# The first x turned into four PSUM banks by halves, and one idle matmul behind the turning where two stood

## The reference, cut to what matters

```python
k = x @ W_lat + b_lat                      # 256 -> 128, one latent shared by all heads, also the values
q = (x @ W_d + b_d) split into 16 heads of 128
att = softmax(causal(q @ k.T / sqrt(128)))
x = layernorm(x + (att @ k, heads joined) @ W_proj + b_proj)
scores = x @ router_weight + router_bias   # the best half of the rows of each batch
x = layernorm(x + scatter(sigmoid(score) * ffn(chosen rows)))
```

## Time and profile before

| what | value |
|---|---|
| median of 3 runs | 280.72 us (280.70 to 280.82) |
| the profiled execution's own time | 280.79 us |
| its span, first to last instruction | 279.1 us |
| PE busy | 271.6 us, 97% of the span |
| DVE busy | 218.8 us, 78% |
| ACT busy | 212.1 us, 76% |
| POOL busy | 153.9 us, 55% |

### The profile page before, as it was taken

One profiled execution on the slowest core, in us unless ns is written; L12 is line 12 of the kernel. 1 busy time (PEld: TensorE's weight loads), 2 busy tenths in 40 slices (PEclk: granted clock), 3 DMA queues, 4 the chain that ended last, 5 costly groups with the idle time before them and its releaser, 6 DMA issues.

```text
span 279.1 us, 6206 instructions
## 1 busy us (share of the span) xinstructions
PE 271.6 (97%) x1885; PEld 247.2 (89%) x1885; DVE 218.8 (78%) x701; ACT 212.1 (76%) x578; POOL 153.9 (55%) x214
## 2 busy tenths in 40 slices
PE   8999999999999999999999999999999999999991
PEld 4878999999999998999999999999999999999990
DVE  2698777777777777788789888899988887779882
ACT  3689877777787778887787877787777778879471
POOL 6468444444443336555666866665657847238652
PEclk9999999999999999999999999999999999999997
DMA  6593111011101111111111111110112200020151
GB/s 184 137 305 112 39 40 34 27 33 38 34 24 36 38 39 38 40 38 42 38 38 40 38 41 38 39 37 22 38 38 79 78 21 21 1 77 1 58 171 38
DMA packets 18842, 15.53 MB, mean 56 GB/s; under 512 B 1641, under 2 KB 18178, under 8 KB 18818
## 3 DMA queue, kind: packets, MB, share of 16 engines
q1 hardware_dynamic: 18242, 13.65, 16.8%
q0 software_dynamic: 576, 1.58, 1.6%
HBM read 12.60 MB, written 2.63 MB: 55 GB/s over the span
## 4 chain that ended last, share of the span: by engine, by line
PE 97%; DVE 0%; POOLq 0%; issue 0%; ACT 0%; DVEq 0%
PE bank L412 21%; PE bank L414 20%; PE bank L413 20%; PE bank L547 9%; PE ps_out L412 7%; PE ps_out L413 6%; PE ps_out L414 6%; PE bank L527 3%; PE bank L637 3%; PE bank L470 1%; PE bank L424 1%; POOLq L60 0%; PE bank L676 0%; PE bank L678 0%; PE bank L557 0%
## 5 line engine op out<-in xcount | busy, mean ns | idle before, releaser
L841 ACT ACTIVATE probs<-probs,negmax 128x512 f32<-128x512 f32 (+3 forms) x128 | 72.6, 576 | 5.7 <-DVE negmax L1026 4.3
L1384 POOL TENSOR_TENSOR wd_hi<-wd_raw,zero 128x256 fp32r<-128x256 f32 x31 | 23.7, 766 | 87.9 <-DVE probs L1098 84.7
L849 ACT CAST pT_hi<-bank 128x512 fp32r<-128x512 f32 (+2 forms) x96 | 43.4, 488 | 28.1 <-PE bank L547 27.7
L1026 DVE CUSTOM_DVE_ANT_0 probs<-bank,mask_row 128x512 f32<-128x512 f32 (+3 forms) x128 | 59.2, 482 | 0.7 <-PE bank L504 0.7
L1035 DVE TENSOR_TENSOR pT_lo<-bank,pT_hi 128x512 fp32r<-128x512 f32 (+2 forms) x96 | 52.8, 552 | 6.1 <-ACT pT_hi L849 5.5
L547 PEld LDWEIGHTS bank<-ident_r,prob_words 128*128 128x128 f32 x310 | 33.0, 140 | 5.5 <-ACT probs L893 0.4
L412 PE MATMUL ps_out<-wp_hi,yT_hi 128*128 128x256 f32 x124 | 37.1, 299 | 0.0
L412 PE MATMUL bank<-kT_hi,qT_hi 128*128 128x256 f32 (+2 forms) x94 | 36.5, 388 | 0.0
L413 PE MATMUL ps_out<-wp_lo,yT_hi 128*128 128x256 f32 x124 | 35.0, 282 | 0.0
L414 PE MATMUL ps_out<-wp_hi,yT_lo 128*128 128x256 f32 x124 | 35.0, 282 | 0.0
L1055 DVE TENSOR_TENSOR yT_lo<-bank,yT_hi 128x512 fp32r<-128x512 f32 x31 | 21.4, 690 | 15.8 <-PE bank L414 13.6
(11 more groups left out here) (203 smaller groups left out, 731.8 us busy)
## 6 DMA issues: line engine op xcount, KB each, us to landing
wd_raw<-in_L_attn_W_d SPq DMA_DIRECT2D x32, 128.0 KB, 2.2
wp_raw<-in_L_attn_W_proj SPq DMA_DIRECT2D x32, 128.0 KB, 2.1
wf_raw<-in_L_ffn_w SPq DMA_DIRECT2D x2, 1024.0 KB, 6.4
x_nat<-in_L_attn_x SPq DMA_DIRECT2D x4, 256.0 KB, 2.9
out<-z_all SPq DMA_DIRECT2D x4, 256.0 KB, 2.3
picked<-ranked SPq DMA_DIRECT2D x2, 258.0 KB, 2.8
wlat_raw<-in_L_attn_W_lat SPq DMA_DIRECT2D x1, 128.0 KB, 3.5
bproj_all<-in_L_attn_b_proj SPq DMA_DIRECT2D x1, 128.0 KB, 3.6
```

What stands on the lines that cost most here:

```text
L841: act.activation(p_tile(s, j), p_tile(s, j), ACT.Exp, bias=negmax[:, s, j:j + 1], scale=-1.0, accum_out=sums[:, s, j:j + 1]).then_inc(exp_ ...
L849: act.copy(pT_hi[:, dst], src).then_inc(pt_hi_done, 1)
L1026: dve.tensor_tensor_reduce(p_tile(s, j), score_bank[j], mask_row[:, (TILES - 1 - j) * P:], -SCALE, -MASKED, ALU.add, ALU.min, accum_out=ne ...
L1384: pool.tensor_tensor(hi, src, nothing, ALU.add).then_inc(hi_done, 1)
```

## The change

The first x is turned into four half banks: the rows' first half goes to `ps_t0` and `ps_t1`, the second to `ps_s2` and `ps_s10`, a chunk in each. `x_turned` is raised for each half of each chunk. ACT makes four copies of 128x256 in place of two of 128x512, DVE four subtractions of 128x256 in place of two of 128x512. The first subtraction stands ahead of DVE's wait for W_lat, the second behind the copy of W_lat, the other two after it. The waits in `project_k_first` count halves. The turned biases go to `ps_s3`, because `ps_s2` is in use. Behind the turning stands one idle matmul. The second x is turned as before, with its counts moved on.

```diff
+        x_banks = [[ps_t0[:, 0:KEEP], ps_t1[:, 0:KEEP]], [ps_s2[:, 0:KEEP], ps_s10[:, 0:KEEP]]]
+
+        def x_half(t, half, c):
+            return t[:, c, half * KEEP:(half + 1) * KEEP]
...
-        WAKING, AWAKE = 6, 2
+        WAKING, AWAKE = 6, 1
...
                     for c in range(CH):
-                        dst = (ps_t0, ps_t1)[c]
+                        dst = (ps_t0, ps_t1)[c][:, half * KEEP:(half + 1) * KEEP] if b else x_banks[half][c]
                         if b and half == 0:
                             pe.wait_ge(x_split, c + 1)
...
-                        if half:
+                        if half or not b:
                             last.then_inc(x_turned, 1)
...
                 pe.wait_ge(wlat_hi_done, 1)
-                pe.wait_ge(x_hi_done, 1)
+                pe.wait_ge(x_hi_done, 3)
                 pe.matmul(ps_kT, w_hi[:, 0, :], x_hi[:, 0, :], start=True, stop=False, skip_group_check=True)
-                pe.wait_ge(x_hi_done, 2)
+                pe.wait_ge(x_hi_done, 4)
                 pe.matmul(ps_kT, w_hi[:, 1, :], x_hi[:, 1, :], start=False, stop=False, skip_group_check=True)
-                pe.wait_ge(x_split, 1)
+                pe.wait_ge(x_split, 3)
                 pe.matmul(ps_kT, w_hi[:, 0, :], x_lo[:, 0, :], start=False, stop=False, skip_group_check=True)
...
-                pe.transpose(ps_s2[:, 0:BIASES], bias_rows[:, :], ident[0:BIASES, 0:BIASES]).then_inc(bias_turned, 1)
-                pe.wait_ge(x_split, CH)
+                pe.transpose(ps_s3[:, 0:BIASES], bias_rows[:, :], ident[0:BIASES, 0:BIASES]).then_inc(bias_turned, 1)
+                pe.wait_ge(x_split, 4)
...
-            def x_high(b):
+            def x_high_halves():
+                for half in range(2):
+                    for c in range(CH):
+                        act.wait_ge(x_turned, CH * half + c + 1)
+                        act.copy(x_half(xT_hi[0], half, c), x_banks[half][c]).then_inc(x_hi_done, 1)
...
-            def x_low(b, c):
-                dve.wait_ge(x_hi_done, CH * b + c + 1)
-                dve.tensor_tensor(xT_lo[b][:, c, :], (ps_t0, ps_t1)[c][:, :],
-                                  xT_hi[b][:, c, :].bitcast(F32), ALU.subtract).then_inc(x_split, 1)
+            def x_low_half(half, c):
+                dve.wait_ge(x_hi_done, CH * half + c + 1)
+                dve.tensor_tensor(x_half(xT_lo[0], half, c), x_banks[half][c],
+                                  x_half(xT_hi[0], half, c).bitcast(F32), ALU.subtract).then_inc(x_split, 1)
...
+            x_low_half(0, 0)
             dve.wait_ge(wlat_in, 16)
             dve.tensor_copy(wlat_hi[:], wlat_raw[:]).then_inc(wlat_hi_done, 1)
+            x_low_half(0, 1)
             for c in range(CH):
-                x_low(0, c)
+                x_low_half(1, c)
             dve.wait_ge(bias_turned, 1)
-            dve.tensor_copy(bias_cols[:, :], ps_s2[:, 0:BIASES]).then_inc(bias_done, 1)
+            dve.tensor_copy(bias_cols[:, :], ps_s3[:, 0:BIASES]).then_inc(bias_done, 1)
```

More of the change, by code:

```diff
@@ L419, in turn_x @@
                     for c in range(CH):
-                        dst = (ps_t0, ps_t1)[c]
+                        dst = (ps_t0, ps_t1)[c][:, half * KEEP:(half + 1) * KEEP] if b else x_banks[half][c]
                         if b and half == 0:
                             pe.wait_ge(x_split, c + 1)
-                        for j in range(2 * half, 2 * half + 2):
+                        for j in range(2):
                             last = pe.transpose(dst[:, j * P:(j + 1) * P].bitcast(F32R),
-                                                x_words[:, b * TILES + j, c * P:(c + 1) * P], ident_r[:, :])
-                        if half:
+                                                x_words[:, b * TILES + 2 * half + j, c * P:(c + 1) * P], ident_r[:, :])
+                        if half or not b:
                             last.then_inc(x_turned, 1)
@@ L451, in project_k_second @@
                 for c in range(CH):
-                    pe.wait_ge(x_split, CH + c + 1)
+                    pe.wait_ge(x_split, 2 * CH + c + 1)
                     last = product(ps_kT, (wlat_hi[:, c, :], wlat_lo[:, c, :]),
@@ L542, in turn @@
                 if at.fixed == 1 and n < CH:
-                    pe.wait_ge(x_split, CH + n + 1)
+                    pe.wait_ge(x_split, 2 * CH + n + 1)
                 a = 0
@@ L798, in split_queries, with x_high_second @@
                                scale=1.0).then_inc(q_hi_done, 1)
-            def x_high(b):
+            def x_high_halves():
[3 more added lines that the diff above has]
+                        act.copy(x_half(xT_hi[0], half, c), x_banks[half][c]).then_inc(x_hi_done, 1)
+            def x_high_second():
                 for c in range(CH):
-                    act.wait_ge(x_turned, CH * b + c + 1)
-                    act.copy(xT_hi[b][:, c, :], (ps_t0, ps_t1)[c][:, :]).then_inc(x_hi_done, 1)
+                    act.wait_ge(x_turned, 2 * CH + c + 1)
+                    act.copy(xT_hi[1][:, c, :], (ps_t0, ps_t1)[c][:, :]).then_inc(x_hi_done, 1)
             def kT_high(b):
@@ L826, in k_high @@
                 act.copy(k_hi[b][:, :, :], ps_ks[b][:, 0:SEQ - P].rearrange("p (j l) -> p j l", l=LAT)).then_inc(k_hi_done, 1)
-            x_high(0)
+            x_high_halves()
             act.wait_ge(wd_in[0], 16)
@@ L834, in _ @@
             kT_bias(0)
-            x_high(1)
+            x_high_second()
             def exps(at, js):
@@ L988, in _, with x_low_second @@
             dve.memset(still[:, :], 0.0).then_inc(still_filled, 1)
-            def x_low(b, c):
-                dve.wait_ge(x_hi_done, CH * b + c + 1)
-                dve.tensor_tensor(xT_lo[b][:, c, :], (ps_t0, ps_t1)[c][:, :],
-                                  xT_hi[b][:, c, :].bitcast(F32), ALU.subtract).then_inc(x_split, 1)
+            def x_low_half(half, c):
+                dve.wait_ge(x_hi_done, CH * half + c + 1)
+                dve.tensor_tensor(x_half(xT_lo[0], half, c), x_banks[half][c],
+                                  x_half(xT_hi[0], half, c).bitcast(F32), ALU.subtract).then_inc(x_split, 1)
+            def x_low_second(c):
+                dve.wait_ge(x_hi_done, 2 * CH + c + 1)
+                dve.tensor_tensor(xT_lo[1][:, c, :], (ps_t0, ps_t1)[c][:, :],
+                                  xT_hi[1][:, c, :].bitcast(F32), ALU.subtract).then_inc(x_split, 1)
             def kT_low(b):
@@ L1069, in period @@
                     if at.fixed == 0:
-                        x_low(1, 0)
-                        x_low(1, 1)
+                        x_low_second(0)
+                        x_low_second(1)
                     wait(dve, scores_ready, p * 3 + 3)
```

## The result

The changed kernel takes 281.25 us in the median of 22 runs (280.94 to 283.12); the kernel before, run beside it, 280.81 us (280.61 to 281.26, 22 runs). The ratio is 1.0026, with a 95% interval from 1.0015 to 1.0036.

The account below looks back on a forecast made before the run. PE was taken as the bound, its start of k held in turn by W_lat, ACT's second copy and DVE's first subtraction. Terms 0.07 - 0 - 0 = +0.07 us gave a median of 280.79, rounded 280.8; range 280.4 to 281.2.

Parts of the forecast that it names:

- The idle matmul: Prologue, PE ahead of k: removing the second idle matmul frees no time, as PE waits for W_lat anyway; 0.
- the clock, and slower: Rival, PE at k and first queries: the clock rises later, 0.20 more per slow 512-column matmul, up to 283.1; chance 0.08.
- The rest: Other prologue work: POOL's products, W_d's copy, the bias transpose, DMAs and queues change nothing; 0.
- ACT's copies and DVE's subtractions: Prologue: k's second matmul gains 0.07, but DVE's order makes the third 0.07 us later than today; +0.07.
- W_lat starts k: Prologue: W_lat's landing, not x, releases k's first matmul, whose weight load stays near 5.63.
- Nothing arrives: Rival, prologue: something fixed holds the bias transpose near 7.17 and swallows the 0.07; 280.72; chance 0.15.
- A small gain: Rival, prologue: x's low half stops binding, k's third matmul follows the second after 0.24; 0.17 won, 280.55; chance 0.08.

Follow-up runs that it names:

- experiment 2: The kernel before with one idle matmul behind the turning in place of two, without the halves; 282.45 us, ratio 1.0054.
- experiment 12: The changed kernel with no idle matmul behind the turning in place of one; 282.47 us, ratio 1.0036.
- 9: The kernel before with two one-column copies more on ACT at the start, into existing tiles; 280.98 us, ratio 1.0006.
- 1: The changed kernel with the second idle matmul put back, halves kept; 281.17 us, ratio 1.0007.
- 5: The kernel before with two one-column copies more on ACT at the start, into a new tile that nobody reads; 281.54 us, ratio 1.0021.
- 6: The changed kernel with two idle matmuls and three one-column copies more on ACT into a new tile; 281.55 us, ratio 1.0022.
- 11: The changed kernel with DVE taking chunk 0 first, one idle matmul more between x's halves, three ACT copies into existing tiles; 280.98 us, ratio 1.0000.
- 3: The changed kernel with one idle matmul more, between the turning of x's halves; 281.20 us, ratio 1.0010.
- 4: The changed kernel with two idle matmuls and DVE's second and third subtraction exchanged, chunk 0 first; 281.22 us, ratio 1.0006.
- 8: The changed kernel with DVE taking chunk 0 first, one idle matmul more between x's halves, three ACT copies into a new tile; 281.62 us, ratio 1.0021.
- 10: The changed kernel with two idle matmuls and three one-column copies more on ACT into existing tiles; 281.02 us, ratio 1.0003.
- 7: The kernel before with an idle matmul more between the turning of x's halves, whole chunks kept; 281.11 us, ratio 1.0004.

## Why the prediction was wrong

Two terms that I put at nothing failed. The idle matmul makes the long executions, and with them more than half of the mean's shift. The other, which I didn't see, lies in the loop and makes most of the median's, the number that was forecast: the sixteen short executions alone have a median of 281.21 us, 0.40 above the kernel before, and the six long ones move it by another 0.04.

- **The idle matmul: wrong, and the step that failed.** I put it at 0 because the second idle matmul lies in the wait for W_lat; so it does, and nothing waits for PE there. But it is also the work that PE does before k. From one execution, in which the rise stood before the second idle matmul, I concluded that the rise would stand there in every execution, "what PE did until then is the same in both kernels". The runs show that the rise is early in some executions and late in others of the same kernel, and that the idle matmul shifts the odds: 6 of 22 above 282, against 0 of 22 beside it (2 of 116 over all runs). This made 0.42 of the 0.75 us of the mean.
- **The rival "the clock, and slower": right as a mechanism, its chance of 0.08 too small, its price about right.** Each matmul at the low level costs 0.20, as forecast; all twelve of k and the queries were slow in experiment 2 (2.9 us with the late x), some seven in the changed kernel's profile (1.49 by the second query matmul). The range should not have left this case out. The Trainium skill, "TensorE: Matmul & The Clock Gate", section "Part 1: The HAM clock gate (the "warmup" mystery)", also says that the number of slow matmuls varies between runs of one kernel. The times here fit that, though each kernel has only one trace: 4 of 12 executions of experiment 12 show no long time and 8 do. I didn't use that sentence.
- **A term that was missing, the other step that failed.** "The rest" counted DMAs and queues, and not that ACT and DVE get two instructions more each ahead of the loop. At the loop's first pass ACT then stands still for 0.3 us, and PE loses 0.21 at 31.4, which 9 makes without halves; near 127 us DVE stands still 0.36 us longer than before, and PE loses 0.09 at 134.5, which only the halves make. The profiled executions of 1 and of the changed kernel show both, 0.30 us together, about what the sixteen short executions lose in the mean (0.33). That sum rests on single traces: a rise within k, as in 5, 6 and 11, may hide in some of the sixteen, and the gain in the prologue differs between executions.
- **ACT's copies and DVE's subtractions: right.** The copies took 0.38 and stood 0.27 apart, the subtractions 0.42 and 0.34; the first one stood ahead of W_lat, done at 5.03 (4.61 + 0.42) before 5.41. The second matmul gained, and the third gave it back. The third's load was released by `xT_lo`, as the forecast had it; the balance, put at +0.07, was +0.03 in experiment 1.
- **W_lat starts k: right in the changed kernel too,** but not always: it started k at 5.52 in experiment 1 and at 5.76 in the changed kernel's profile, and where it landed before DVE asked for it, as in 12, k waited for ACT's copy ([0.30 <-ACT xT_hi L809]). The 0.12 us between the first three runs of the kernel before said too little on how executions differ: its 22 lie 0.65 us apart.
- **"Nothing arrives": refuted as a mechanism.** The bias transpose (L448) came at 7.09 in experiment 1, 0.08 earlier than in the earlier trace rows, together with the matmul ahead of it. Nothing fixed holds it near 7.17.
- **"A small gain": real in the prologue, lost behind it.** With W_lat early the third matmul of k in 3 follows the second after 0.23 (5.90 and 6.13), as this rival has it, and the queries start 0.25 ahead of the earlier trace rows; the order that would bring it with W_lat late (4, 8, 11) moved no time that the runs resolve. What was won, the loop took back.

What decides in a single execution whether the rise is early stays open. x's second half came late in the profiles of the changed kernel, of 2 and of 4, all three long; in 12 it came on time and the rise was late as well; in 10 PE idled 0.41 us just ahead of k, behind two idle matmuls, and the execution was short; in 11 the rise came within k. The clock records in the traces begin with the rise, and agree with the steps: it stands at 5.29 us in the kernel before, between 3.7 and 6.9 in the nine other short ones, and at 9.32 (the changed kernel), 10.10 (4), 10.26 (12) and 12.89 (2) in the long ones, none between. Why ACT stands still is open too: shown is only that two further instructions bring the standstill to the loop's entry, and that three more take it from there. The instruction queue among the profile's DMA queues gives a hint: with ACT's old count and with two more, one of its 8 KB transfers starts 0.6 to 1.1 us behind that copy of `yT` (30.40 before, 32.02 in the changed kernel), and in the four kernels with five more none does; there two stand at 26.6 to 26.9, where the others have one. That the loading of the program makes the standstill is not tested.

## What to carry to other kernels

An idle matmul that is hidden on the critical path can still be paying for the clock of what follows; before taking it out, look at more than one execution, because one profile shows one outcome of something that differs between executions. Where times fall into two groups, compare counts of the long ones, not only medians: the median here moved 0.44 us while one execution in four lost 1.5. And an edit on an engine that isn't the bound can cost at a place that it doesn't touch: compare the starts of the same instructions all along the trace, and try the bare number of instructions by itself.

## What the runs showed that I had not expected

- The granted-clock column printed 1.00 for 5.30 to 9.30 in the changed kernel, while 512-column matmuls stood 0.43 apart. The trace's clock record begins only with the rise, at 9.32; the steps show the level ahead of it, the column doesn't.
- Six idle matmuls at the start, eight transposes, and one more idle matmul: the same program came out at 280.94 or at 283.12.
- ACT's standstill of 0.3 us at the loop's entry depends on how many instructions ACT had before: with two more (1, 3, 4, 5, 9, 12 and the changed kernel) it is there, with none more (the kernel before, 2, 7) or five more (6, 8, 10, 11) it isn't; with five more ACT stands still near 178 us and PE's step comes at 186.0. The step at 134.5 goes with the halves and a standstill of DVE.
- A new tile of 12 bytes for each partition that only idle copies write slowed PE by 0.35 to 0.42 us over 231 us, in three pairs of kernels.
